# A two-block transformer kernel on one core: the first group of x in two transfers and over three engines, the ada products behind V, and part of the zero fill in the first MLP

## The reference, cut to what matters

```
# block 0
h = film(rmsnorm(x), cond)                     # x*(1+scale)+shift, from cond @ film1
x = x + (softmax(Q K^T / sqrt(128)) V) @ proj + proj_b
x = x + gelu(film(rmsnorm(x), cond) @ w1 + b1) @ w2 + b2
# block 1
mod = silu(cond) @ ada_w.T + ada_b             # 6 pieces: shift, scale, gate, twice
x = x + gate * attention(modulate(layernorm(x)), mask)     # 16 heads of 8
x = x + gate * (gelu_tanh(modulate(layernorm(x)) @ fc1 + b) @ fc2 + b)
```

## Time and profile before

| | us |
|---|---|
| median of 3 runs | 183.45 (182.68 to 183.99) |
| the profiled execution's own time | 183.18 |
| its span in the trace | 181.4 |
| PE busy | 173.0 (95%) |
| DVE, ACT, POOL busy | 122.4 (67%), 113.1 (62%), 100.3 (55%) |

### The profile page before, as it was taken

The page is one execution under the profiler, slowest core; times in us unless marked ns, Lnnn a source line. Parts: engine busy times, 40 slices in busy tenths (PEclk is TensorE's granted clock), DMA queues, the critical chain, the costliest instruction groups (busy, mean ns, idle before and its releaser), DMA issues.

```text
span 181.4 us, 5682 instructions
## 1 busy us (share of the span) xinstructions
PE 173.0 (95%) x2250; PEld 133.1 (73%) x2250; DVE 122.4 (67%) x374; ACT 113.1 (62%) x243; POOL 100.3 (55%) x187
## 2 busy tenths in 40 slices
PE   6989999999999999999999989999999999999994
PEld 6866876778476698878778866787678765768593
DVE  6899869859306269585776777887788855661334
ACT  7426786793972830577757766676866878946600
POOL 8939999878850205934546642975087466470000
PEclk9999999999999999999999999999999999999999
DMA  4993000211900300101011001010000000001103
GB/s 105 405 411 129 4 0 14 62 26 58 405 0 4 117 0 5 60 5 63 1 63 63 5 4 63 6 65 2 5 5 2 5 5 0 4 0 58 61 0 116
DMA packets 4277, 10.91 MB, mean 60 GB/s; under 512 B 540, under 2 KB 1260, under 8 KB 3948
## 3 DMA queue, kind: packets, MB, share of 16 engines
q1 hardware_dynamic: 3788, 8.83, 13.6%
q10 hardware_dynamic: 464, 1.73, 2.5%
HBM read 7.24 MB, written 1.09 MB: 46 GB/s over the span
## 4 chain that ended last, share of the span: by engine, by line
PE 81%; POOL 11%; DVE 4%; ACT 2%; issue 2%; POOLq 0%; DVEq 0%
PE ps L305 16%; PE ps L292 13%; PE ps L359 10%; PE ps L340 9%; PE ps L376 8%; POOL xn L1109 3%; POOL xb L1095 3%; PE ps L386 3%; PE ps L433 3%; POOL rstd L1090 2%; PE ps L230 2%; PE ps L396 2%; PE ps L317 2%; PE ps L324 2%; PE ps L391 2%; PE ps L320 2%
## 5 line engine op out<-in xcount | busy, mean ns | idle before, releaser
L976 DVE TENSOR_REDUCE nm<-ps 128x8 f32<-128x1024 f32 x32 | 37.7, 1218 | 8.7 <-PE ps L340 8.7
L696 ACT ACTIVATE shared<-ps 128x1024 f32<-128x1024 f32 x32 | 31.0, 1021 | 15.3 <-PE ps L359 15.3
L1090 POOL TENSOR_TENSOR rstd<-var_eps,half 128x4 f32<-128x4 f32 x16 | 16.3, 1018 | 36.0 <-DVE var_eps L820 19.2
L305 PEld LDWEIGHTS ps<-W,hid 128*128 128x128 f32 x256 | 29.6, 192 | 1.7 <-issue 1.4
L305 PE MATMUL ps<-W,hid 128*128 128x128 f32 x256 | 30.3, 276 | 0.0
L292 PE MATMUL ps<-hT,W 128*128 128x512 f32 x56 | 25.9, 596 | 0.0
L663 ACT ACTIVATE hid<-ps,W 128x512 f32<-128x512 f32 x28 | 18.2, 695 | 6.7 <-PE ps L292 6.7
L340 PEld LDWEIGHTS ps<-k_pad,q_pad 32*128 32x128 f32 x512 | 15.8, 186 | 8.3 <-issue 7.8
L622 ACT ACTIVATE hT<-ps,shift,scale 128x128 f32<-128x128 f32 x44 | 16.9, 466 | 7.1 <-PE ps L230 7.1
L340 PE MATMUL ps<-k_pad,q_pad 32*128 32x128 f32 x512 | 18.8, 283 | 1.4 <-ACT shared L696 1.4
L359 PE MATMUL ps<-q_pad,k_pad 32*128 32x128 f32 x512 | 18.8, 282 | 0.5
(11 more groups left out here) (132 smaller groups left out, 321.3 us busy)
## 6 DMA issues: line engine op xcount, KB each, us to landing
gate<-gates SPq DMA_DIRECT2D x1, 2048.0 KB, 6.9
xs<-x SPq DMA_DIRECT2D x4, 256.0 KB, 5.3
gate<-mask ACTq DMA_DIRECT2D x1, 1024.0 KB, 10.2
q_pad<-apT SPq DMA_DIRECT2D x4, 256.0 KB, 2.4
k_pad<-apT SPq DMA_DIRECT2D x4, 256.0 KB, 2.6
W<-weights SPq DMA_DIRECT2D x1, 768.0 KB, 11.2
out<-xs SPq DMA_DIRECT2D x3, 256.0 KB, 2.4
W<-weights SPq DMA_DIRECT2D x1, 512.0 KB, 7.5
```

Of the source, the lines that this page charges most:

```text
L305: ins = mm(bank(o_bank)[:, j], hid[g % 2][:, f, j], w(w2, C, C * f), start=(f == 0), stop=(f == FC - 1), skip_group_check=True)
L696: a(pT[b % 2][:, 2 * e:2 * e + 2], ps[:, 4 * e:4 * e + 2, :].rearrange("n r (t q) -> n r t q", t=4), ACT.Exp, scale=HD ** -0.5).then_inc(s ...
L976: v.tensor_reduce(nm[b % 2][:, 8 * e:8 * e + 8], ps[:, 2 * e:2 * e + 2, :].rearrange("n r (t k) -> n (r t) k", t=4), AX.X, ALU.max, negate ...
L1090: p.tensor_tensor(rstd[:, k, G * g:G * g + G], var_eps[:, k, G * g:G * g + G], half[:, 0:G], ALU.pow)\
```

## The change

- **Transfer.** The first group of x comes in two transfers of two sequences (`x_in0`, `x_inb`) and DVE's statistics wait for each half.
- **Normalising.** Of group 0, POOL does sequence 0, ACT 1 and 2, DVE 3; of group 1, POOL does 0 and 1, ACT 2 and 3. ACT waits for POOL's `rstd` (`a_pow`) for both.
- **PE's order.** The four ada products leave their place ahead of q and k of group 0 and stand behind V, in another bank. Their four bias additions on DVE move from behind the statistics of group 1 to ahead of the gate rows, and wait with these for one semaphore. DVE's row sums of group 1 move behind `a_affine(0)`.
- **Zero fill.** DVE and ACT clear only half of `q_pad[:, 1]` and `q_pad[:, 3]` at the start, and the other halves later: ACT behind the gelus of stage b's group 1, DVE behind `pbias1`. POOL's first fill is 44 of 48 rows; the rest of it and the last tile come behind `norm(1, 0)`. `clear_v(0)` takes the place of `clear_v(1)`, and `clear_v(1)` comes behind `root(2, 1)`. The four counts of `pad_zero` are given at the ends of: ACT's late half, DVE's late half, POOL's first and POOL's last fill.

SP's list is the same but for the one transfer more at its start.

```
@@ sync
-            sp.dma_start(xs[:, 0:G], x[:, 0:G]).then_inc(s["x_in0"], 16)
+            sp.dma_start(xs[:, 0:2], x[:, 0:2]).then_inc(s["x_in0"], 16)
+            sp.dma_start(xs[:, 2:G], x[:, 2:G]).then_inc(s["x_inb"], 16)
@@ tensor
                 if g == 0:
                     pe.wait_ge(s["a_xn0"], 1)
+                    pe.wait_ge(s["a_xa"], 1)
+                if g == 1:
+                    pe.wait_ge(s["a_xd"], 1)
...
-            pe.wait_ge(s["w_ada"], 16)
-            pe.wait_ge(s["silu_ok"], 1)
-            pe.wait_ge(s["film_ok"], 2)
-            for n, j in enumerate((1, 4, 0, 3)):
-                ins = mm(ps[:, 7, B * n:B * n + B], w("ada", C, C * j), silu[:], start=True, stop=True,
-                         skip_group_check=True)
-            ins.then_inc(s["ada_mm"], 1)
             a_qk(0, 0)
             a_qk(0, 1)
             a_value(0)
-            pe.wait_ge(s["ada_ok"], 1)
+            pe.wait_ge(s["w_ada"], 16)
+            pe.wait_ge(s["silu_ok"], 1)
+            for n, j in enumerate((1, 4, 0, 3)):
+                mm(ps[:, 6, C + B * n:C + B * n + B], w("ada", C, C * j), silu[:], start=True, stop=True,
+                   skip_group_check=True)
+            pe.wait_ge(s["film_one"], 4)
             a_norm(1)
...
-            pe.wait_ge(s["c_vinit"], 4)
+            pe.wait_ge(s["c_vinit"], 2)
@@ scalar
-            a(q_pad[:, 3].rearrange("p b n -> p (b n)"), spare[:].broadcast_to((N, B * N)), ACT.Copy)\
-                .then_inc(s["pad_zero"], 1)
+            a(q_pad[:, 3, 0:8].rearrange("p b n -> p (b n)"), spare[:].broadcast_to((N, 8 * N)), ACT.Copy)
...
+            act.wait_ge(s["a_pow"], 1)
+            for b in (1, 2):
+                ins = a(xn[0][:, b], xs[:, b], ACT.Copy, scale=rstd[:, 0, b:b + 1])
+            ins.then_inc(s["a_xa"], 1)
             act.wait_ge(s["film_ok"], 2)
             affine("a_", 0, 0, bank(0), range(2))
             act.wait_ge(s["wvp_mm"], 1)
             a(wvp[:], ps[:, 6, 0:C], ACT.Copy).then_inc(s["wvp_ok"], 1)
+            act.wait_ge(s["x_in1"], 16)
+            act.wait_ge(s["a_pow"], 2)
+            for j in (2, 3):
+                ins = a(xn[1][:, j], xs[:, G + j], ACT.Copy, scale=rstd[:, 0, G + j:G + j + 1])
+            ins.then_inc(s["a_xd"], 1)
             a_kv(0)
...
             gelus("b_", 1, ACT.Gelu, "cols0", COL["mlp_b1"], 0)
+            a(q_pad[:, 3, 8:16].rearrange("p b n -> p (b n)"), spare[:].broadcast_to((N, 8 * N)), ACT.Copy)\
+                .then_inc(s["pad_zero"], 1)
             affine("b_", 3, 1, bank(4))
@@ vector
-            v.memset(q_pad[:, 1].rearrange("p b n -> p (b n)"), 0.0).then_inc(s["pad_zero"], 1)
+            v.memset(q_pad[:, 1, 0:8].rearrange("p b n -> p (b n)"), 0.0)
...
+            dve.wait_ge(s["a_pow"], 1)
+            v.tensor_scalar(xn[0][:, 3], xs[:, 3], rstd[:, 0, 3:4], None, ALU.mult).then_inc(s["a_xn0"], 1)
...
-            row_sums(0, 1)
             a_affine(0)
-            statistics(0, 1, rows=False)
-            dve.wait_ge(s["ada_mm"], 1)
-            for n, j in enumerate((1, 4, 0, 3)):
...
+            statistics(0, 1)
             a_q(0)
...
-            dve.wait_ge(s["gate_mm"], 1)
+            dve.wait_ge(s["ada_mm"], 1)
+            for n, j in enumerate((1, 4, 0, 3)):
...
             v.tensor_tensor(gate_rows[:].rearrange("b g c -> b (g c)"), ps[0:B, 6, 2 * C:4 * C], row("gate_b", 2 * C)[0:B, :],
...
             v.tensor_tensor(pbias1[:], ps[:, 7, 3 * C:4 * C], row("proj1_b"), ALU.add).then_inc(s["pbias_ok"], 1)
+            v.memset(q_pad[:, 1, 8:16].rearrange("p b n -> p (b n)"), 0.0).then_inc(s["pad_zero"], 1)
@@ gpsimd
-            p.memset(k_pad[:, 0:3].rearrange("p t b n -> p (t b n)"), 0.0).then_inc(s["pad_zero"], 1)
+            p.memset(k_pad[:, 0:3].rearrange("p t b n -> p (t b n)")[:, 0:44 * N], 0.0).then_inc(s["pad_zero"], 1)
...
-                for j in range(2 if k == 0 and g == 0 else G):
+                for j in range(1 + g if k == 0 and g < 2 else G):
...
-            for q in range(0, B, 4):
-                ins = p.memset(k_pad[:, 3, q:q + 4].rearrange("p b n -> p (b n)"), 0.0)
-            ins.then_inc(s["pad_zero"], 1)
...
-            clear_v(0)
             norm(1, 0, "b_")
+            p.memset(k_pad[:, 2, 12:16].rearrange("p b n -> p (b n)"), 0.0)
+            for q in range(0, B, 4):
+                ins = p.memset(k_pad[:, 3, q:q + 4].rearrange("p b n -> p (b n)"), 0.0)
+            ins.then_inc(s["pad_zero"], 1)
             next_bias(0)
             norm(1, 1, "b_")
             norm(1, 2, "b_")
-            clear_v(1)
+            clear_v(0)
...
             root(2, 1, s["c_pow"])
+            clear_v(1)
+            ones_v(1)
```

More of the change, by code:

```diff
@@ L141, in build @@
         names = """x_in0 x_in1 x_in2 x_in3 w_film w_attn0 w_ada w_mlp0 w_block1 rows_in mask_in mask_rin gate_out gate_in y_out
-            ident_ok half_ok spare_ok stats_ok film_mm a_hd pb_mm gate_mm film_one film_ok silu_e silu_one silu_ok
+            ident_ok half_ok spare_ok stats_ok film_mm x_inb a_hd a_xa a_xd pb_mm film_one film_ok silu_e silu_one silu_ok
             ada_mm ada_ok gate_ok  wvp_mm wvp_ok bias_ok bcol_ok pbias_ok pad_zero aug_ok aug_out aug_in maskb_ok c_vinit
@@ L370, in weighted @@
                 pe.wait_ge(s["c_v"], b // G + 1)
+                if b == G:
+                    pe.wait_ge(s["c_vinit"], 4)
                 v = vx[b // G % 2][:, b % G].rearrange("n (e j s c) -> n e j s c", e=2, j=4, s=2)
@@ L464, in _ @@
                          skip_group_check=True)
-            ins.then_inc(s["gate_mm"], 1)
+            ins.then_inc(s["ada_mm"], 1)
             for g in range(3):
@@ L639, in a_exp @@
                       accum_out=aden[:, u, j:j + 1]).then_inc(s["a_exp"], 1)
+            act.wait_ge(s["x_in0"], 16)
+            act.wait_ge(s["x_inb"], 16)
+            act.wait_ge(s["a_pow"], 1)
+            for b in (1, 2):
+                ins = a(xn[0][:, b], xs[:, b], ACT.Copy, scale=rstd[:, 0, b:b + 1])
+            ins.then_inc(s["a_xa"], 1)
             act.wait_ge(s["film_ok"], 2)
@@ L687, in front_v @@
                 act.wait_ge(s["c_V"], g + 1)
+                if g == 1:
+                    act.wait_ge(s["c_vinit"], 3)
                 v = ps[:, V_BANK[g], :].rearrange("n (a k d) -> n a k d", k=2, d=HD)
@@ L758, in _ @@
                 front_h(b)
-            act.wait_ge(s["c_vinit"], 2)
+            act.wait_ge(s["c_vinit"], 1)
             front_v(0)
@@ L798, in row_sums @@
                 for j in range(G):
+                    if k == 0 and g == 0 and j == 2:
+                        dve.wait_ge(s["x_inb"], 16)
                     v.bn_stats(bn[:, j], xs[:, G * g + j]).then_inc(s["stats_ok"], 1)
@@ L853, in _ @@
             v.tensor_tensor(silu[:], w("cond", B), cond_r[:], ALU.mult).then_inc(s["silu_ok"], 1)
[L854 to L857, removed]
             def a_q(g):
@@ L915, in _ @@
             statistics(0, 3)
-            dve.wait_ge(s["gate_mm"], 1)
+            dve.wait_ge(s["ada_mm"], 1)
+            for n, j in enumerate((1, 4, 0, 3)):
+                dst = scale[:, 2 + n, :] if n < 2 else shift[:, n, :]
+                ins = v.tensor_scalar(dst, ps[:, 6, C + B * n:C + B * n + B], col("cols1", COL1["ada"] + j),
+                                      1.0 if n < 2 else 0.0, ALU.add, ALU.add)
+            ins.then_inc(s["ada_ok"], 1)
             v.tensor_tensor(gate_rows[:].rearrange("b g c -> b (g c)"), ps[0:B, 6, 2 * C:4 * C], row("gate_b", 2 * C)[0:B, :],
@@ L1154, in _, with ones_v @@
             next_bias(1)
-            pool.wait_ge(s["c_vinit"], 2)
-            for t in vx:
+            def ones_v(u):
+                pool.wait_ge(s["c_vinit"], 2 * u + 1)
                 for k in range(2):
-                    z = t[:].rearrange("n b (a z) -> n (b a) z", z=64)[:, :, 48 * k + HD:48 * k + HD + 1]
+                    z = vx[u][:].rearrange("n b (a z) -> n (b a) z", z=64)[:, :, 48 * k + HD:48 * k + HD + 1]
                     ins = p.memset(z, 1.0)
                 ins.then_inc(s["c_vinit"], 1)
+            ones_v(0)
             def front_x(b):
```

## The result

The changed kernel takes 193.04 us (median of 6 runs, 192.09 to 194.34), the kernel before 183.38 beside it (6 runs, 182.68 to 184.01): a ratio of 1.0548 [1.0517, 1.0579]. It is slower by 9.7 us where 8.3 were forecast, and 0.04 us above the end of the range. The profiled execution took 193.81, with a span of 192.0 against 181.4. Medians here are over all runs of a kernel; ratios leave out disturbed executions.

The account below looks back on a forecast made before the run. It took PE, busy for 95% of the span, to bound the kernel. To the profiled 183.18 us it added 6.3 for the delay of `scores(0)`, front's gain included, and 2.0 for PE's slow restart: 191.5 us, range 188.3 to 193.0.

Parts of the forecast that it names:

- The front: PE up to the first turn of stage b: 0.85 us earlier, 0.1 plus 0.75, bounds 0 and 1.65.
- SP's start: First transfer of SP's list after four counts of `pad_zero`, the last from ACT's late half: at 48.35 us, 20.7 later.
- Gate rows landed: SP's wait for the 16 KB behind three spreads: issued 3.3 after SP's first transfer, 8.7 to land, so 60.4 us.
- the third rival: Quicker spreads in SP's queue hide the late fills: not slower, 182.3 us, or 181.5 with the front's upper bound; chance 0.06.
- The broadcast: The 2 MB of gates in SP's queue ahead of q and k: 6.9 us to landing, at 67.3.
- net delay of `scores(0)`: PE's stall of 7.1 us for q and k, landing at about 68.6, makes `scores(0)` 6.3 us later.
- The upper bound of 7.4: Delay of `scores(0)` if q and k wait for the whole gate broadcast and then take a full 2.4 us.
- The restart: PE's products behind the stall run slowly after its rest: 2.0 us, from 20 x (0.231 - 0.132).
- The first rival: The stall before `scores(0)` without a slow restart of PE: 189.5 us, chance 0.22.
- Costed at nothing: Fills behind `norm(1, 0)`, POOL's two `vx` fills less before stage c, ACT's late fill in idle time: 0 us.
- Rival 2: q and k pass the gates in SP's queue and land at 64.0: 184.8 us, up to 187; chance 0.09.
- The fourth: More than the sum, by a longer slow restart or a held-up late half on ACT: 193 to 195 us, chance 0.05.

Follow-up runs that it names:

- the first experiment: Changed kernel with the gate rows, the wait for their landing and the gate broadcast moved ahead of SP's wait for `pad_zero`: 183.53 us, ratio 1.0018.
- The holding experiment: Changed kernel, but SP waits for the gate broadcast to land before issuing q and k of the first group: 193.79 us, ratio 1.0589.
- the spin experiment: Changed kernel with 28 spin products on PE ahead of its wait for the mask terms: 192.25 us, ratio 1.0535; run again, 1.0461 beside 1.0544 without.

## Why the prediction was right in its mechanism and wrong in its size

- **The front**: forecast 0.85, measured 1.04 at the first turn of stage b. The give-back at the softmax came as foreseen: 0.18 gained where 0.1 was forecast, with DVE's statistics again at 1.21 beside POOL's addition (the line below) and the gate rows at 19.44 + 0.40. At the first turn the number is luck: it came at 8.73, where the spin products were forecast to hold it until 8.67, but in this execution they ended at 7.71, and the turn waited 1.01 for ACT's `xn`.

```profile
17.73 1.21 DVE L836 SCALAR_TENSOR_TENSOR var_eps<-agg,mean_sq 128x4 f32<-128x4 f32 x1
```

- **SP's start**: forecast 48.35, measured 48.62, released by ACT's `q_pad`.
- **Gate rows landed**: forecast 60.4, measured 60.38. The three spreads were as slow at 50 us as at 30 (8.41 for 8.7), which settles the third rival; the 1.4 of the first experiment speaks for the spreads ahead of the gate rows as what makes this landing long.
- **The broadcast: this step failed.** The sum took 6.9 for it, the time of a broadcast that had the engines to itself; here it took 8.4, because q and k ran beside it. From 62 to 66 us 344 GB/s were moved, 403 in the main part of before's. k landed 1.26 behind it, as forecast (1.3), but at 70.06 and not at "about 68.6". So the net delay of `scores(0)` is 7.75 where 6.3 stood in the sum: 1.45 short. The forecast treated the queue as strictly one after the other in the order of landing (right) and in the use of the engines (wrong). The holding experiment shows it: from the broadcast's issue to k landed the forecast had 8.2, the broadcast's time alone and only 1.3 for q and k behind it, and no order gives both. Side by side it was 9.7, one after the other 10.2. The upper bound of 7.4 was exceeded for the same reason.
- **The restart**: forecast 2.0, measured 2.9 in the first profile and 1.8 in two others of the change. Its sign and place were right, and the spin experiment shows that it is PE's state and not the data. That the size came near is in part luck: it was an estimate from spin passes at the start, 0.231 each, in stretches whose granted clock reads 1.00, and the slow blocks behind the hole ran at 0.50. What no row of before shows is now a row: granted clock 0.51 and 0.50 from 66 to 76 us, with 1.00 until 66 and 1.00 again from 77 on. The start is another case: PE had done nothing before it either and its passes are slow, but the granted clock from 1.5 to 6 us reads 1.00; why they are slow, no run shows. The first rival, no slow restart, falls with the measured restart.
- **Sum**: by medians 9.66 against 8.3. The missing 1.36 is about the broadcast's term, 1.45, with a restart near the forecast 2.0; that is an estimate, since only profiled executions show the restart. By the two profiles it is 10.6: 1.45 from the broadcast and 0.9 from a long restart.
- **Costed at nothing, wrongly**: POOL's fills of `vx`. The forecast counted two less before stage c, but the clearing of the second buffer only moved, to 59.26, beside DVE's `xc`, and made that 2.49 for 1.12. In the change the stall hides it (the turn waits 1.08, but q and k are later still); once the stall was cured, the same wait stood ahead of `scores(0)` and took about what the front had gained. Two of DVE's groups were longer beside POOL's work: `var_eps` with 1.21 beside its addition, `xc` with 2.49 beside its fills. They took 0.16 and 1.12 when they no longer stood beside it; what in POOL's work makes them longer, no run shows.
- Rival 2 was wrong in its time (k did not land ahead of the gates), though right in that q and k shared the engines with them. The fourth, 193 to 195, has the time, but not by its causes alone: ACT's fill was not held up, and the broadcast's longer time is not among them.

## What to carry to other kernels

When a step is moved that a queue's issuing engine waits for, walk that queue's whole list from the new time: 1 us of zero fill, put where ACT had time for it, cost 10 us because a wait for a 16 KB landing and a 2 MB transfer stood between it and the next data that PE needed. Put transfers whose use is far away, and the waits for them, ahead of the wait that may come late, or leave the early fill alone. Work moved into an idle stretch of an engine was not free here (DVE's `xc` took 2.49 us beside POOL's moved fills, for 1.12): look for what the other engines run at the new place.

## What the runs showed of the hardware

- In the first profile of the change PE was idle from about 63 us on; its granted clock stood at half from 66, and at full again from 77, after products had run from 70.20 on. The cost was 1.8, 1.8 and 2.9 us in three profiles of the change, 1.9 and 3.0 in two variants with the same hole. With spin products in the pause the granted clock reads 1.00 from 62 to 81 us and the two blocks behind it take the 4.98 of before, in two profiles.
- The same 12 spin passes at the start took 1.58 or 2.91 us in different executions of one kernel.
- A 16 KB transfer issued behind three spreads of 128 KB each landed 8.1 to 9.3 us after its issue in ten profiles, whenever they ran, and 1.4 us after it in three with the spreads behind it. The spreads moved some 50 to 60 GB/s (55 in before at 33 to 36 us, 60 in the change at 53 to 58).
- The 2 MB broadcast took 7.1 us with q and k held back (6.9 in before) and 8.4 in the change, with their 512 KB behind it in the same queue; the two transfers of those 512 KB took 8.6 each in the change, for 2.5 and 2.4 held back.
- DVE's four scalings into `xc` took 2.49 or 2.50 us beside POOL's fills in seven profiles and 1.66 in an eighth, for 1.12 in before and 1.11 or 1.12 in the four others without the fills there.
